# The second layer of a decoder rebuilt in pairs of sequences, its context side moved into the experts' loop, and new bank use in both attentions of the first layer

## The reference

```python
x = x + L0_attn(ln(x))        # five SSM layers, then causal self-attention: 16 heads of 64
x = x + L0_xattn(ln(x), ctx)  # cross-attention: 16 heads of 16, with biases
x = x + L0_ffn(ln(x))         # experts: top 2 of 8, silu(x Wg) * (x Wu) Wd
# second layer
z = ln(x);  q, k, v = z Wq^T, z Wk^T, z Wv^T
x = x + softmax(q k^T / 16) v                      # one head of 256
q = ln(ln(x)) * w1 + b1;  k, v = ln(ctx) * w2 + b2, ln(ctx) * w3 + b3
x = x + ln(softmax(q k^T / factor) v) * w4 + b4
z = ln(x); zq, wq = int8 by row maxima, int8 by column maxima
x = x + (zq wq) * row scale * column scale
```

## Time and profile before

| | us |
|---|---|
| median of 3 runs | 1473.04 |
| the three runs | 1471.09, 1473.04, 1576.78 |
| the profiled execution | 1469.42 |
| its span, first to last instruction | 1467.7 |
| busy in the span: TensorE / VectorE / GpSimd / ScalarE | 1207.2 / 824.6 / 672.0 / 635.4 |

### The profile page before, as it was taken

One profiled execution on the slowest core, in us unless ns is written; L12 is line 12 of the kernel. 1 busy time (PEld: TensorE's weight loads), 2 busy tenths in 40 slices (PEclk: granted clock), 3 DMA queues, 4 the chain that ended last, 5 costly groups with the idle time before them and its releaser, 6 DMA issues. The chain is left out here.

```text
span 1467.7 us, 21516 instructions
## 1 busy us (share of the span) xinstructions
PE 1207.2 (82%) x7243; PEld 945.4 (64%) x7243; DVE 824.6 (56%) x1847; ACT 635.4 (43%) x1863; POOL 672.0 (46%) x659
## 2 busy tenths in 40 slices
PE   4999999999699999998557777764999999377632
PEld 3888888888577777776446666653666666266521
DVE  6888888888434544444355655445222222237885
ACT  2555555555245454545225556541222222256520
POOL 2276767675512332424354444431466665224531
PEclk9999999999899999999977888775999999699865
DMA  4001010100000000000070001133223222400000
GB/s 145 1 15 55 15 54 15 54 15 15 0 1 1 1 1 1 1 1 1 1 265 1 2 0 37 52 128 98 36 44 48 47 44 42 139 15 15 15 15 29
DMA packets 36925, 53.75 MB, mean 37 GB/s; under 512 B 8192, under 2 KB 30720, under 8 KB 35296
## 3 DMA queue, kind: packets, MB, share of 16 engines
q1 hardware_dynamic: 27808, 39.14, 7.8%
q0 software_dynamic: 8736, 10.25, 4.3%
q10 hardware_dynamic: 288, 3.15, 0.6%
HBM read 40.78 MB, written 11.74 MB: 36 GB/s over the span
## 5 line engine op out<-in xcount | busy, mean ns | idle before, releaser
L414 DVE SCALAR_TENSOR_TENSOR ssm_conv<-bank,conv_w,ssm_conv 128x508 f32<-128x508 f32 (+2 forms) x240 | 159.2, 729 | 9.7 <-ACT ssm_conv L350 9.7
L1503 PE MATMUL bank<-expert_raw,e_rows_t 128*128 x312 | 148.3, 599 | 1.2 <-ACT e_rows_t L1575 1.2
L303 PE MATMUL bank<-w_out,ssm_u 128*128 128x256 f32 x640 | 143.5, 382 | 0.0
L710 ACT ACTIVATE a_prob<-bank,a_neg_max 128x128 f32<-128x128 f32 x256 | 90.7, 368 | 100.6 <-DVE a_neg_max L751 100.6
L303 PEld LDWEIGHTS bank<-w_out,ssm_u 128*128 128x128 f32 x640 | 119.9, 190 | 17.9
L1180 ACT ACTIVATE expert_raw<-bank,x_neg_max 128x128 f32<-128x128 f32 x256 | 91.1, 379 | 83.0 <-DVE x_neg_max L1114 83.0
L808 POOL TENSOR_TENSOR a_prob<-a_prob,a_inv 128x512 f32<-128x512 f32 x64 | 66.3, 1042 | 131.4 <-DVE a_inv L756 131.3
L1038 POOL TENSOR_TENSOR expert_raw<-expert_raw,x_inv 128x512 f32<-128x512 f32 x64 | 66.9, 1045 | 115.5 <-DVE x_inv L1120 115.5
L1715 DVE COPY e_h_t<-bank 128x512 f32<-128x512 f32 x39 | 27.0, 692 | 128.1 <-PE bank L1512 128.1
L1437 POOL DMA_INDIRECT x_rows<-e_y,e_index x39 | 62.9, 1613 | 75.1 <-ACT e_y L1588 72.1
L508 POOL TENSOR_TENSOR act_t_lo<-ssm_turned,act_t_hi 128x512 fp32r<-128x512 f32 x40 | 51.6, 1290 | 97.5 <-ACT ssm_turned L375 97.5
(11 more groups left out here) (368 smaller groups left out, 3214.0 us busy)
## 6 DMA issues: line engine op xcount, KB each, us to landing
expert_raw<-in_experts_laid SPq DMA_DIRECT2D x6, 1536.0 KB, 10.8
attn_raw<-in_attn_w_laid SPq DMA_DIRECT2D x4, 1024.0 KB, 7.5
w_in_raw<-in_L_attn_in_proj_w SPq DMA_DIRECT2D x5, 640.0 KB, 8.5
expert_raw<-in_experts_laid ACTq DMA_DIRECT2D x2, 1536.0 KB, 8.7
w_out<-in_L_attn_out_proj_w SPq DMA_DIRECT2D x5, 512.0 KB, 3.4
x_res<-in_x SPq DMA_DIRECT2D x4, 512.0 KB, 5.5
expert_raw<-in_ctx_t_laid SPq DMA_DIRECT2D x4, 512.0 KB, 6.7
z_rows<-e_z SPq DMA_DIRECT2D x4, 512.0 KB, 10.2
```

The source lines that it names most:

```text
L303: mm = pe.matmul(UWY[h][:, s * D:(s + 1) * D], u[:, g % 2, c, t:t + P], w_out[:, c, :], start=(c == 0), stop=(c == KI - 1))
L414: op = dve.scalar_tensor_tensor(out=acc, in0=xs, scalar=conv_w[:, c, TAPS - 1 - back:TAPS - back], in1=acc, op0=ALU.mult, op1=ALU.add)
L710: e = act.activation(prob[:, m % 4, i, :], S[m % 2][:, i * P:(i + 1) * P], ACT.Exp, bias=neg_max[:, m % 4, i:i + 1], accum_out=total[:, m ...
L1503: mm = pe.matmul(bank[:, :], rows_t[:, t % 2, k, :], W[:, bass.ds(at + (column + k * FFN), FFN)], start=(k == 0), stop=(k == KD - 1))
```

## The change

**Self-attention.** The mask matmuls go. VectorE adds the mask while it copies the scores from the bank to `prob`; maxima and exponentials read `prob`. TensorE waits for that copy (`masked`) ahead of the next scores, no longer for the exponentials.

**Cross-attention.** Four S banks for two; one job bank for two; OT and Y in one bank for all sequences. Scores wait for the exponentials of three ticks back, each job for the copy of the job ahead of it, and the output for the addition of the sequence ahead. A score matmul takes both key halves at once, 256 columns. `OUT` and `ADD` come one tick earlier.

**Experts' loop.** The context is loaded into the memory of z, and cv is made in place; ck_t takes that of z_t, and the second layer's weights that of lane_hot. In tiles 1 to 8 VectorE measures two sequences each. In tiles 14 to 29 one sequence each is normed on ScalarE, turned on TensorE into the free half of ZT's bank, copied with its gains on ScalarE into ck_t, and turned into values by two VectorE operations. From tile 31 VectorE quantises the last weight in steps. SyncE loads X behind the last add of rows, in eight pieces, inside this stage; no clearing block follows.

**Second layer.** q k^T = z (Wq^T Wk) z^T: one product of the weights ahead of the loop, one projection q, and z_t itself as keys. All products of this layer are single fp32 matmuls. ln(ln(x)) becomes one norm: the variance is widened to v (1 + eps) + eps^2. The cross-attention's softmax sum isn't divided out; the norm behind it takes eps times its square in place of eps. Rounding is one addition of a large constant, with its subtraction inside the copy of the turned tile, and no clipping. All norms are applied by ScalarE. There are eight pairs in place of four groups, one PSUM bank for each use, and each queue is sorted by `CHAIN[phase] + 65 * pair`.

```diff
                     if m >= 2:
-                        pe.wait_ge(exp_ready, m)
-                    for par in range(2):
-                        pe.matmul(S[par][:, :], mem["ident_bf"][:, :], mem["causal"][:, :].unsqueeze(1).broadcast_to([P, 4, P]),
-                                  start=True, stop=False, skip_group_check=True)
+                        pe.wait_ge(masked, m)
...
-                        e = act.activation(prob[:, m % 4, i, :], S[m % 2][:, i * P:(i + 1) * P], ACT.Exp,
+                        e = act.activation(prob[:, m % 4, i, :], prob[:, m % 4, i, :], ACT.Exp,
...
+                    if m >= 4:
+                        dve.wait_ge(pt_ready, m - 3)
+                    dve.tensor_tensor(prob[:, m % 4, :, :], S[m % 2][:, :].rearrange("p (i k) -> p i k", i=4),
+                                      mem["causal"][:, :].unsqueeze(1).broadcast_to([P, 4, P]), ALU.add).then_inc(masked, 1)
+                    dve.wait_ge(masked, m + 1)
+                    dve.tensor_reduce(neg_max[:, m % 4, :], prob[:, m % 4, :, :], AX.X, ALU.max,
                                       negate=True).then_inc(max_ready, 1)
...
-    S, JOB, PT = psum[0:2], psum[2:4], psum[4:6]
-    OT = lambda b: psum[6 + b % 2][:, 0:D]
-    Y = lambda b: psum[6 + b % 2][:, D:2 * D]
+    S, PT, JOB = psum[0:4], psum[4:6], psum[6]
+    OT, Y = psum[7][:, 0:D], psum[7][:, D:2 * D]
...
-    INVERT, TURN, MEAN, SPLIT_HIGH, SPLIT_LOW, OUT, ADD = 1, 3, 5, 9, 9, 11, 12
+    INVERT, TURN, MEAN, SPLIT_HIGH, SPLIT_LOW, OUT, ADD = 1, 3, 5, 9, 9, 10, 11
...
@@ -1241,15 +1250,15 @@
                     if m % GROUP_TICKS == 0:
                         pe.wait_ge(k_copied, G * KD + KD)
                         pe.wait_ge(q_copied, G * KD + KD)
-                    if m >= 2:
-                        pe.wait_ge(exp_ready, m)
-                    for i in range(4):
+                    if m >= TILES:
+                        pe.wait_ge(exp_ready, m - TILES + 2)
+                    for c in range(KD):
                         for r in (first, first + 1):
                             rows = slice(r * ROWT, (r + 1) * ROWT)
-                            mm = pe.matmul(S[r % 2][:, i * P:(i + 1) * P], q_t[rows, G % 2, i // 2, step * P:(step + 1) * P],
-                                           k_t[G % 2][rows, i % 2, i // 2, step * P:(step + 1) * P], start=True, stop=True,
+                            mm = pe.matmul(S[r][:, c * 2 * P:(c + 1) * 2 * P], q_t[rows, G % 2, c, step * P:(step + 1) * P],
+                                           k_t[G % 2][rows, :, c, step * P:(step + 1) * P], start=True, stop=True,
                                            tile_position=(r * ROWT, 0))
-                            if i == 3:
+                            if c == KD - 1:
                                 mm.then_inc(s_ready, 1)
...
@@ -1265,15 +1274,15 @@
                     G, s = divmod(b, GS)
                     if s == 0:
                         pe.wait_ge(v_copied, G * KD + KD)
-                    if b >= 2:
-                        pe.wait_ge(y_added, b - 1)
+                    if b >= 1:
+                        pe.wait_ge(y_added, b)
...
     CONSTS = 11
+    C_TURN = 14
+    turns_context = lambda t: C_TURN <= t < C_TURN + SEQS
...
+            sp.dma_start(wf[:, :, :], io["rhs_laid"]).then_inc(l_loaded, 16)
+            last = SLOT_TILES - 1
+            sp.wait_ge(y_sent[last % 3], 16 * (last // 3) + 16)
+            for G in range(PAIRS):
+                sp.dma_start(X[:, G * PAIR:(G + 1) * PAIR, :], x_rows[G * PT:(G + 1) * PT].rearrange(
+                    "(b t) d -> t b d", t=P)).then_inc(mem["x_loaded"][G], 16)
+            sp.wait_ge(l_loaded, 64)
...
+                    pool.wait_ge(c_var_ready, 1)
+                    pool.tensor_tensor(c_rstd[:, :], c_rstd[:, :], mem["neghalf"][:, :], ALU.pow).then_inc(c_rstd_ready, 1)
...
+                if turns_context(t - 1):
+                    pe.wait_ge(ck_copied, (t - C_TURN) * KD)
+                if turns_context(t):
+                    pe.wait_ge(cn_ready, t - C_TURN + 1)
+                    for k in range(KD):
+                        tr = pe.transpose(CT[:, k * P:(k + 1) * P], cn[:, t % 2, k * P:(k + 1) * P], ident[:, :])
...
+            def normalise_context(b):
+                if b == 0:
+                    act.wait_ge(c_shift_ready, 1)
+                if b >= 2:
+                    act.wait_ge(ct_ready, b - 1)
+                act.activation(cn[:, (C_TURN + b) % 2, :], context[:, b, :], ACT.Identity, bias=c_shift[:, b:b + 1],
+                               scale=c_rstd[:, b:b + 1]).then_inc(cn_ready, 1)
...
+            def value_of_context(b):
+                dve.wait_ge(cn_ready, b + 1)
+                if b == 0:
+                    dve.wait_ge(p_loaded, 96)
+                dve.scalar_tensor_tensor(out=wt[:, b % KD, :], in0=context[:, b, :], scalar=c_mv[:, b, 0:1], in1=rows4[:, 0, :],
+                                         op0=ALU.subtract, op1=ALU.mult).then_inc(cv_ready, 1)
+                dve.wait_ge(cv_ready, 2 * b + 1)
+                dve.scalar_tensor_tensor(out=cv[:, b, :], in0=wt[:, b % KD, :], scalar=c_rstd[:, b:b + 1], in1=rows4[:, 1, :],
+                                         op0=ALU.mult, op1=ALU.add).then_inc(cv_ready, 1)
+
+            done = [0]
...
+CHAIN = {name: at for at, name in (
+    (0, "measure_a"), (12, "invert_a"), (27, "norm_a"), (36, "turn_a"), (42, "copy_zt"), (48, "project_q"), (49, "project_v"),
+    (67, "copy_q"), (69, "copy_v"), (74, "scores"), (84, "maxima"), (89, "exps"), (97, "invert_sums"), (98, "turn_probs"),
+    (101, "copy_probs"), (106, "outputs"), (116, "add"), (127, "measure_x"), (139, "invert_x"), (154, "norm_x"), (163, "add_b4"),
+    (164, "turn_x"), (170, "copy_cq"), (180, "cscores"), (190, "cmaxima"), (195, "cexps"), (203, "square_sums"), (204, "turn_cprobs"),
+    (207, "copy_cprobs"), (212, "coutputs"), (222, "measure_o"), (235, "invert_o"), (252, "norm_o"), (262, "gain_o"), (276, "add_o"),
+    (284, "measure_f"), (296, "invert_f"), (311, "norm_f"), (320, "scale_f"), (332, "quantise"), (340, "turn_f"), (347, "copy_f"),
+    (354, "multiply"), (362, "store"), (372, "add_f"))}
+APART = 65
+
+
+def in_turn(*phases):
+
+    places = sorted((CHAIN[phase] + APART * G, G, phase) for phase in phases for G in range(PAIRS))
+    return [(phase, G) for _, G, phase in places]
...
+def pair_invert(pool, norm, G, neg_one):
+
+    at = slice(G * PAIR, (G + 1) * PAIR)
+    pool.wait_ge(norm["var_ready"], G + 1)
+    pool.tensor_tensor(norm["neg_mean"][:, at], norm["mv"][:, at, 0], neg_one[:, :], ALU.mult).then_inc(norm["neg_mean_ready"], 1)
+    pool.tensor_tensor(norm["ve"][:, at], norm["ve"][:, at], norm["neghalf"][:, 0:PAIR], ALU.pow).then_inc(norm["rstd_ready"], 1)
+    pool.wait_ge(norm["neg_mean_ready"], G + 1)
+    pool.wait_ge(norm["rstd_ready"], G + 1)
+    pool.tensor_tensor(norm["shift"][:, at], norm["neg_mean"][:, at], norm["ve"][:, at], ALU.mult).then_inc(norm["shift_ready"], 1)
+
...
+def pair_apply(act, norm, G, row, out):
+
+    act.wait_ge(norm["shift_ready"], G + 1)
+    for i in range(PAIR):
+        b = G * PAIR + i
+        act.activation(out(i), row(i), ACT.Identity, bias=norm["shift"][:, b:b + 1],
+                       scale=norm["ve"][:, b:b + 1]).then_inc(norm["z_ready"], 1)
...
+    TR, Q, S, O, CT, CS, CO, F = psum
+    V, PROB_T, CPROB_T = TR, S, CS
...
+                for j in range(KD):
+                    mm = pe.matmul(Q[:, i * D:(i + 1) * D], wq[:, j, i * P:(i + 1) * P], wk[:, j, :], start=(j == 0), stop=(j == KD - 1))
+            mm.then_inc(qk_ready, 1)
...
+                    pe.wait_ge(zt_copied, G + 1)
+                    if G == 0:
+                        pe.wait_ge(qk_copied, 1)
+                    else:
+                        pe.wait_ge(q_copied, G)
+                    for k in range(KD):
+                        for j in range(KD):
+                            mm = pe.matmul(Q[:, k * PT:(k + 1) * PT], qk[:, j, k * P:(k + 1) * P], z_t[:, G % 2, j, :],
+                                           start=(j == 0), stop=(j == KD - 1))
+                    mm.then_inc(q_ready, 1)
+                elif phase == "project_v":
+                    pe.wait_ge(zt_copied, G + 1)
+                    for s in range(PAIR):
+                        for j in range(KD):
+                            mm = pe.matmul(V[:, s * D:(s + 1) * D], z_t[:, G % 2, j, s * P:(s + 1) * P], wv[:, j, :],
+                                           start=(j == 0), stop=(j == KD - 1))
+                    mm.then_inc(v_ready, 1)
+                elif phase == "scores":
+                    pe.wait_ge(q_copied, G + 1)
...
-                                                 op0=ALU.subtract, op1=ALU.mult).then_inc(og_ready, 1)
-                    dve.wait_ge(og_ready, G * GS + GS)
-                    dve.wait_ge(norm_o["rstd_ready"], G + 1)
```

(15 more changed lines are left out.)

823 lines of the change are left out of this document (382 added, 441 removed).

## The result

The changed kernel takes 1384.43 us (median of 4 runs, 1383.81 to 1390.17) against 1472.47 for the kernel before on the same chip: a ratio of 0.941, 95% interval 0.938 to 0.945. The profiled execution took 1383.8 us with a span of 1382.1, 85.6 less than the 1467.7 before. One run of the kernel before, at 1576.78 us, fell in a slower state and doesn't enter the ratio. The forecast was 1325, range 1286 to 1375: right in sign, and some 60 us too hopeful.

What follows compares the result with a forecast made beforehand. Self-attention and experts' loop were taken as bound by TensorE instructions, cross-attention and second layer by waits between engines; 1469.4 - 26 - 38 + 4.5 - 4.7 - 83 = 1322, forecast as 1325 us, range 1286 to 1375.

Steps and rivals of the forecast that it cites:

- TensorE: 56 matmuls and turns, 6.3 at the upper clock: Second layer: TensorE's work for one pair of sequences, 6.3 us at the upper clock, twice that at the lower.
- a 512-column fp32 matmul starts 0.43 us apart from the next: Trace reading from the experts' loop: 0.43 us per fp32 matmul, against 0.69 for three fp32r ones in the second layer.
- the rule to which I gave hardly a chance: Second layer: true FP32 takes four passes, giving TensorE some 12 us a pair and making it the bound.
- rival (c): Second layer: four-pass rule, 12.5 us of TensorE a pair in place of 10.1, total 1345 us; chance 0.02.
- rival (b): Waits change name: cross-attention in step through single banks, second layer's output bank sets 13 us a pair; 1377 us, chance 0.25.
- The four banks, put at 50: Cross-attention: four score banks let scores run ahead, gaining 50 us over 16 ticks of the last group and 48 others.
- the 2.45 us for a tick with jobs: Cross-attention's loop: 2.45 us a tick in the 48 ticks before the last group, against 3.25 before the change.
- Two neighbouring jobs collide in each of three groups, 2 us each: Cross-attention's loop: two turns collide in the one job bank; with the output bank's 0.1 us per sequence, 7 us.
- one copy of 0.6: Head of cross-attention: seven hand-overs of 0.6 us for the copy and 0.1 or 0.2 for the wait, 5 us.
- I let 4 us of the 14 remain: Self-attention: of TensorE's 14.0 us of waits for exponentials ahead of the scores, 4 stay and 10 are gained.
- The cover of three ticks: Self-attention: a probability tile's turn follows its scores by three ticks of 4.3 us, covering VectorE's new additions.
- VectorE and ScalarE over 65% busy: Second layer, sign of being right: both engines over 65% busy, the end about 116 us after its start.

Runs made afterwards that it cites:

- l_one_pass: The changed kernel with fp32r operands for q, v, scores and outputs of the second layer's self-attention; 1372.24 us, ratio 0.935.

## Why the prediction was right in sign and wrong in size

**Second layer (-57.8, forecast -83, bounds 60 to 97).** The step that failed is the term "TensorE: 56 matmuls and turns, 6.3 at the upper clock", and under it the reading of the earlier trace rows: "a 512-column fp32 matmul starts 0.43 us apart from the next". That row shows x4 for what the source writes as two matmuls; 39 tiles of four such matmuls are 156, and the profile counts 312. An fp32 matmul leaves two records. So 512 columns cost 0.86 us, and 256 cost 0.46, as the layer itself shows (the count is of 32 matmuls in the source):

```profile
L2062 PE MATMUL bank<-l_z_t,l_qk x64: 379/379/634, 1248.4 to 1335.3; 128*128 128x256 f32 x64
```

against 0.23 for one fp32r matmul of 512 columns. One fp32 matmul is dearer than the three fp32r ones it replaces (0.86 against 0.69). This is the rule to which I gave hardly a chance: the Trainium skill says in "FP8 and Floating Point Precision", TensorE Precision Notes, that true FP32 takes four passes. The trace agrees: 4 x 0.23 = 0.92, and 0.86 was measured. `l_one_pass` shows the count by itself, 32 records for the same 32 matmuls.

Only fp32 products double. The turns and the last, bf16, product leave one record for each operation of the source. So TensorE's work for a pair is about 10 us at the upper clock, neither the 6.3 of the sum nor the 12.5 of rival (c): with q and v later it is busy for 9.8 us of a round of 11.0 at a granted clock of 1.00; in the kernel after for 12.1 of 14.0, at 0.88.

```profile
1286.57:1297.56 10.99, 9.82 (x63) 8.24 (x61) 9.38 (x35) 9.07 (x25) 7.09 (x15) 1.00 0.01 1
```

Rival (c) had the mechanism, and its chance of 0.02 rested on a miscounted row; its time, 1345, was too low, as it left every other term at its forecast. Behind the first three, the pairs came 12.1 to 14.2 us apart. With the work or its order mended the layer fell by 16 to 18 us, with both by 20: that much of the 25 is TensorE's work where it stood in the chain. The remaining 5 (121.5 against 116.6) stand against later pairs at 11 to 12 us where I had 10.1; VectorE's work was right (9.2 to 9.4 us a round), its packing was not, as the chain runs through ScalarE's and TensorE's queues too. Which item would have to move to shorten it isn't tried. The output bank of rival (b) doesn't hold them: TensorE's waits name no wait for the norm behind it in any of these runs.

**Cross-attention, loop (-16.7, forecast -43).** Two terms. The four banks, put at 50, are worth 25 to 28. The term that was too good is the 2.45 us for a tick with jobs: it came to 3.05, and to 2.74 with the jobs apart, while ticks without jobs took 2.1 against 2.0. Why ticks with jobs don't go faster wasn't isolated: ScalarE still waits 64 us for maxima, but moving these changed nothing. "Two neighbouring jobs collide in each of three groups, 2 us each" named the right wait at half its size (4.1 us) and left out what queues behind it: the neighbours cost 17 to 19 us, where I had 6 or 7 for all single banks in the loop. The drain behind the last scores took 4 us more as well. **Head (+10, forecast +5).** The hand-overs cost 1.5 to 1.8 us for keys and turns, since two operations follow each other or VectorE follows ScalarE, and I had charged one copy of 0.6.

**Self-attention (-17.2, forecast -26, bounds 12 to 31).** The mask matmuls brought 10.8 and not 16.6 over the whole stage. "I let 4 us of the 14 remain" is true by name (2.4 remain) and false in sum: 10.9 turned up in front of the turns (2.2 before). The cover of three ticks was too thin by 1.1 us where jobs stand in VectorE's queue.

**Right.** Experts' loop: from first turn to last down product 231.5 before, 235.0 after, +3.5 against +4.5. Way into the second layer: -5.5 against -4.7; the load of X is issued at 1236.12 and the layer starts at 1240.58. No clearing stands between them. VectorE's 10.1 us a pair: 79 us for eight. Of the signs named ahead, VectorE and ScalarE over 65% busy didn't come (55% and 53% of the layer), and a single bank, the job bank, does head TensorE's waits in cross-attention, which I had named as a sign of being wrong. Rival (b), at 1377, was the nearest case (-20, -15, +6, -5, -58), partly by luck: its mechanism was right in cross-attention, where the single job bank mattered, and wrong in the second layer, where the 12 to 14 us a pair came from TensorE's dearer products in the chain and not from the output bank.

## What to carry to other kernels

Before a duration is read off a grouped row, divide the records by the operations that the source issues: here x64 stood for 32, and the error took a load of 10 us a pair for 6.3. A single bank costs not its copy but every step of the hand-over (1.5 to 1.8 us here where 0.6 was charged), and much less when its users are spread; so spread them, and use all banks while the rest of the stage hasn't begun. In queues ordered by hand, ask for each wait what independent work of the same engine could stand between the two items: moving two phases by three places brought as much as making four of the products three times cheaper, and moving another turn to a place where its neighbours' inputs came late cost 9 us.

## What was not expected of the hardware

Taking work from TensorE went with a lower clock: in the stretch 1280 to 1320 the granted clock was 1.00 with TensorE busy for 35.9 of 40 us and 0.83 to 0.87 with 28 to 30, so part of the saved work was paid back (a 512-column fp32r matmul is recorded with 0.63 us at the lower level and 0.40 at the upper). An exponential that reads the copy in on-chip memory isn't faster than one that reads the bank, but 0.02 us slower on average (groups by line, before and after; busy, mean ns, idle before); the masking addition takes 0.68 us, as the nearest rows had it.

```profile
L710 ACT ACTIVATE a_prob<-bank,a_neg_max 128x128 f32<-128x128 f32 x256 | 90.7, 368 | 100.6 <-DVE a_neg_max L751 100.6
```
```profile
L707 ACT ACTIVATE a_prob<-a_prob,a_neg_max 128x128 f32<-128x128 f32 x256 | 99.7, 391 | 118.7 <-DVE a_neg_max L753 118.4
L750 DVE TENSOR_TENSOR a_prob<-bank,causal 128x512 f32<-128x512 f32 x64 | 43.6, 681 | 1.6 <-PE bank L646 1.6
```
